# First rows of the experts gathered, and their down weights loaded, in the last steps of the attention: a transformer block on one Trainium2 core

## The reference

```python
xn = layernorm(x)                      # x: 4 x 1024 tokens, 256 wide, float32
# attention: 16 heads of 16, causal, with ALiBi bias
q, k, v = xn @ Wq, xn @ Wk, xn @ Wv
w = softmax((where(causal, q @ k.T, -1e30) + slope * (j - i)) / sqrt(16))
attn = (w @ v) @ Wo + bo
# experts: 8 of them, each token goes to its best 2
logits = rms_normalised(xn) @ router_logits
choices = top2(logits); weights = softmax(logits) / sum of the chosen
h = gelu(xs @ w_gate[e]) * (xs @ w_up[e])       # xs: rows sorted by expert, hidden width 256
ffn = sum over the token's 2 choices of weight * scale[e] * (h @ linear[e])
out = x + attn + ffn
```

## Time and profile before

| what | us |
|---|---|
| median of 3 runs | 894.63 (894.17 to 898.16) |
| the profiled execution | 894.28 |
| its span, first to last instruction | 892.5 |
| PE, DVE, ACT, POOL busy | 816.1, 555.9, 491.2, 397.1 |
| mean granted clock of PE | 0.965 |

### The profile page before, as it was taken

How to read it: one execution, slowest core, us unless ns; L and a number is a source line. 1 busy time by engine, 2 the same in 40 slices (tenths; PEclk the granted TensorE clock), 3 DMA queues, 4 the chain that set the end, 5 groups by cost and what they waited for, 6 DMA issues and landing times. The chain is left out here.

```text
span 892.5 us, 17183 instructions
## 1 busy us (share of the span) xinstructions
PE 816.1 (91%) x5618; PEld 422.1 (47%) x5619; DVE 555.9 (62%) x1560; ACT 491.2 (55%) x1011; POOL 397.1 (44%) x478
## 2 busy tenths in 40 slices
PE   4999878999998999999999999849999999999598
PEld 2555413334443344444444444315556555565597
DVE  4777399999999988888888887002222222222287
ACT  1444303777776777777877777823333333333374
POOL 6666301111211245433555421234666666665397
PEclk9999957999999999999999999969999999999699
DMA  8899767766535775567665500056222222222485
GB/s 195 275 290 279 248 84 94 90 72 84 65 50 59 85 100 84 84 87 110 85 91 84 70 2 7 1 169 226 83 86 84 82 83 87 82 85 68 143 251 186
DMA packets 93631, 100.25 MB, mean 112 GB/s; under 512 B 32700, under 2 KB 74300, under 8 KB 93500
## 3 DMA queue, kind: packets, MB, share of 16 engines
q1 hardware_dynamic: 84600, 80.40, 45.8%
q0 software_dynamic: 8960, 18.95, 6.8%
HBM read 63.89 MB, written 35.00 MB: 111 GB/s over the span
## 5 line engine op out<-in xcount | busy, mean ns | idle before, releaser
L825 ACT ACTIVATE probs<-spsum 128x512 f32<-128x512 f32 x576 | 317.5, 602 | 145.1 <-PE spsum L898 138.3
L664 DVE CUSTOM_DVE_ANT_0 junk<-mpsum,mask 128x128 bf16<-128x128 f32 (+7 forms) x512 | 359.1, 754 | 45.3 <-issue 29.6
L872 PE MATMUL mpsum<-ks,qs 102*128 102x512 bf16 (+3 forms) x768 | 183.7, 343 | 28.6 <-DVE maxima L664 22.0
L898 PE MATMUL spsum<-qs,ks 105*128 105x512 bf16 (+3 forms) x768 | 198.1, 329 | 4.8 <-ACT probs L825 3.4
L644 POOL TENSOR_SCALAR_AFFINE_SELECT probs<-probs 128x512 f32<-128x512 f32 x128 | 79.2, 638 | 252.6 <-ACT probs L825 252.3
L918 PE MATMUL cpsum<-probs,vs 128*17 128x256 f32 (+2 forms) x2560 | 154.0, 361 | 1.5 <-POOL probs L644 0.8
L1100 PE MATMUL gu<-w_gu,xTs 128*128 x288 | 137.4, 600 | 1.7 <-ACT xTs L1044 1.7
L1079 DVE COPY hT<-hp 128x256 f32<-128x256 f32 x72 | 30.6, 425 | 165.8 <-PE hp L1107 165.8
L872 PEld LDWEIGHTS mpsum<-ks,qs 102*128 102x128 bf16 x768 | 67.5, 100 | 111.7 <-DVE maxima L664 55.4
L898 PEld LDWEIGHTS spsum<-qs,ks 105*128 105x128 bf16 x768 | 66.9, 97 | 90.8 <-ACT probs L825 39.2
L1019 POOL DMA_INDIRECT expert_rows<-y,places x72 | 70.8, 984 | 69.9 <-ACT y L1053 69.6
(11 more groups left out here) (122 smaller groups left out, 708.5 us busy)
## 6 DMA issues: line engine op xcount, KB each, us to landing
qk_parts<-ctxT SPq DMA_DIRECT2D x32, 384.0 KB, 3.6
qs<-qk_parts SPq DMA_DIRECT2D x96, 128.0 KB
ks<-qk_parts SPq DMA_DIRECT2D x96, 128.0 KB
yk<-expert_rows SPq DMA_DIRECT2D x32, 256.0 KB, 3.0
v_rows<-ctxT SPq DMA_DIRECT2D x8, 544.0 KB, 3.6
vs<-v_rows SPq DMA_DIRECT2D x16, 272.0 KB, 11.0
ctxT<-in_x SPq DMA_DIRECT2D x8, 512.0 KB, 6.2
xn_rows<-ctxT SPq DMA_DIRECT2D x8, 512.0 KB, 5.7
```

The costliest lines, as they stand in the source:

```text
L664: last = dve.tensor_tensor_reduce(junk[:, slot, c:c + w], mpsum[:, slot, c:c + w], keep["mask"][:, S - w:S], 1.0, 3 * NEG, ALU.add, ALU.ma ...
L825: act.activation(probs[:, u % PRING, h], spsum[:, SCORE_AT["S", n, h] % SRING], ACT.Exp, scale=SCALE).then_inc(exp_done, 1)
L872: last = pe.matmul(mpsum[:, slot, at + c:at + e], qs[hq][0:R_MAX, h, qt * P:(qt + 1) * P], ks[hq][0:R_MAX, h, c:e], start=True, stop=True)
L898: last = pe.matmul(spsum[:, SCORE_AT["S", n, h] % SRING, c:c + w], ks[hq][:, h, kt * P:(kt + 1) * P], qs[hq][:, h, q0:q0 + w], start=True, ...
```

## The change

The query and key stacks of all quads become one tensor `stacks`, held for the whole program. The experts' down weights, row buffers and `y` buffers are laid in the stacks of quads 0 and 1: the down weights fill the stack of quad 0, which is read for the last time in step 12, rows and y lie in that of quad 1, read for the last time in step 13. SP loads the down weights in step 13 and the map in step 14; POOL gathers the first four tiles at the end of its attention stream, before the stage ends. AHEAD is now 4, for these gathers and for POOL's loop in `experts`, whose own first gathers are gone. The last stage's rows of x are laid in the stacks of quads 2 and 3, and its working buffers in the gate and up weights' place and over the down weights, rows and y. The diff, without the buffers of the last stage:

```diff
@@ -90,6 +90,10 @@
 SRING = 3
 
 
+RR = 4
+AHEAD = 4
+
+
 PAIRS = 2 * NU
 PV_AT = [[] for _ in range(PAIRS)]
 for _u in range(NU):
@@ -157,13 +161,13 @@
 SCORE_SEQ, SCORE_AT = score_slots()
 
 
-def head_buffers(nc, ctx):
+def head_buffers(nc, ctx, stacks):
 
     sb = lambda name, shape, dt=F32: ctx.enter_context(nc.sbuf_tensor(name, shape, dt))
     sem = lambda name: ctx.enter_context(nc.semaphore(name))
     return {
-        "qs": [sb(f"qs{i}", [ROWS, 4, S], BF16) for i in range(NQ)],
-        "ks": [sb(f"ks{i}", [ROWS, 4, S], BF16) for i in range(NQ)],
+        "qs": [stacks[0:ROWS, i, 0] for i in range(NQ)],
+        "ks": [stacks[0:ROWS, i, 1] for i in range(NQ)],
         "vs": [sb(f"vs{i}", [P, KT, 4, VW]) for i in range(NQ)],
         "stack_in": [sem(f"stack_in{i}") for i in range(NQ)],
         "v_in": [sem(f"v_in{i}") for i in range(NQ)],
@@ -515,6 +519,13 @@
             chunks(pe, body)
 
 
+def gather_rows(pool, scratch, keep, s):
+
+
+    pool.indirect_dma_start(keep["rows"][:, s % RR], None, scratch["xn"],
+                            bass.IndirectOffsetOnAxis(ap=keep["places"][:, s, 0:1].bitcast(U32), axis=0)).then_inc(keep["rows_in"][s % RR], 16)
+
+
 def attend(nc, ins, scratch, keep, heads):
@@ -603,8 +614,15 @@
                 if has(3):
                     sp.wait_ge(pv_done, PRING + NU * t)
                     load_quad(sp, scratch, heads, *quad(b, hq, 3))
+                if t == B * NQ - 3:
+                    sp.wait_ge(pv_done, PRING + NU * t)
+                    for e in range(NE):
+                        sp.dma_start(keep["w_down"][:, e * DH:(e + 1) * DH], ins["w_down"][:, e * DH:(e + 1) * DH]).then_inc(keep["w_down_in"], 16)
                 if has(1):
                     maxima_rows(t + 1, (hq + 1) % NQ)
+                if t == B * NQ - 2:
+                    sp.wait_ge(entries_out, 16 * 2 * NT)
+                    sp.dma_start(keep["places"][:, :, :].rearrange("p s c -> p (s c)"), scratch["map"].rearrange("(p s) c -> p (s c)", p=P)).then_inc(keep["places_in"], 16)
                 if t == MAP_FROM:
                     sp.wait_ge(routed, 1)
                 if MAP_FROM <= t < MAP_FROM + NE:
@@ -612,8 +630,6 @@
                     sp.dma_start(keep["w_gu"][:, e * DH:(e + 1) * DH], ins["w_gu"][:, e * DH:(e + 1) * DH]).then_inc(keep["w_gu_in"], 16)
 
             steps(sp, body)
-            sp.wait_ge(entries_out, 16 * 2 * NT)
-            sp.dma_start(keep["places"][:, :, :].rearrange("p s c -> p (s c)"), scratch["map"].rearrange("(p s) c -> p (s c)", p=P)).then_inc(keep["places_in"], 16)
 
         @block.gpsimd
         def _(pool):
@@ -646,6 +662,10 @@
 
             mask_unit(0, 0)
             steps(pool, body)
+            wait_apart(pool, pv_done, PRING + NU * (B * NQ - 2))
+            wait_apart(pool, keep["places_in"], 16)
+            for s in range(AHEAD):
+                gather_rows(pool, scratch, keep, s)
 
         @block.vector
         def _(dve):
@@ -960,26 +980,20 @@
 def experts(nc, ins, scratch, keep, last_weights):
 
 
-    RR = 4
-    AHEAD = 6
     with ExitStack() as ctx:
         sb = lambda name, shape, dt=F32: ctx.enter_context(nc.sbuf_tensor(name, shape, dt))
         sem = lambda name: ctx.enter_context(nc.semaphore(name))
         w_gu = keep["w_gu"]
-        w_down = sb("w_down", [P, NE * DH, D])
-        rows = sb("rows", [P, RR, D])
-        places, places_in = keep["places"], keep["places_in"]
+        w_down, rows, y, places = keep["w_down"], keep["rows"], keep["y"], keep["places"]
+        w_in, rows_in = keep["w_down_in"], keep["rows_in"]
         xT = sb("xTs", [P, 2, DH, P])
         gate = sb("gate", [P, 2, HID])
         hid = sb("hid", [P, 2, HID])
         hT = sb("hT", [P, 2, DH, P])
-        y = sb("y", [P, RR, D])
         tp = ctx.enter_context(nc.psum_tensor("tp", [P, 2, CH], F32))
         gu = ctx.enter_context(nc.psum_tensor("gu", [P, 2, CH], F32))
         hp = ctx.enter_context(nc.psum_tensor("hp", [P, 2, CH], F32))
         yp = ctx.enter_context(nc.psum_tensor("yp", [P, 2, CH], F32))
-        w_in = sem("w_in")
-        rows_in = [sem(f"rows_in{i}") for i in range(RR)]
         y_out = [sem(f"y_out{i}") for i in range(RR)]
         y_free, passed = sem("y_free"), sem("passed4")
         tp_ready, xT_ready = sem("tps_ready"), sem("xTs_ready")
@@ -997,8 +1011,6 @@
         @block.sync
         def _(sp):
             sp.sem_inc(y_free, RR)
-            for e in range(NE):
-                sp.dma_start(w_down[:, e * DH:(e + 1) * DH], ins["w_down"][:, e * DH:(e + 1) * DH]).then_inc(w_in, 16)
             sp.dma_start(last_weights["w_o"][:, :, :], ins["w_o"]).then_inc(last_weights["in"], 16)
             sp.dma_start(last_weights["bias"][:, :], ins["bo"].partition_broadcast(P)).then_inc(last_weights["in"], 16)
             x_rows = ins["x"].rearrange("(g p) d -> p g d", p=P)
@@ -1011,8 +1023,7 @@
 
                 if s >= RR:
                     pool.wait_ge(tp_ready, s - RR + 1)
-                pool.indirect_dma_start(rows[:, s % RR], None, scratch["xn"],
-                                        bass.IndirectOffsetOnAxis(ap=places[:, s, 0:1].bitcast(U32), axis=0)).then_inc(rows_in[s % RR], 16)
+                gather_rows(pool, scratch, keep, s)
 
             def scatter(s):
                 pool.wait_ge(y_ready, s + 1)
@@ -1024,9 +1035,6 @@
                 pool.wait_ge(y_out[s % RR], 16 * (s // RR + 1))
                 pool.sem_inc(y_free, 1)
 
-            pool.wait_ge(places_in, 16)
-            for s in range(AHEAD):
-                gather(s)
             for s in range(NST):
                 if s >= RR - 1:
                     landed(s - RR + 1)
@@ -1331,6 +1340,9 @@
             "escale": sb("escale", [P, NE]),
             "w_gu": sb("w_gu", [P, NE * DH, 2 * HID]),
             "ctxT": sb("ctxT", [P, B * NQ, S]),
+            "stacks": sb("stacks", [P, NQ, 2, 4, S], BF16),
+            "w_down_in": ctx.enter_context(nc.semaphore("w_down_in")),
+            "rows_in": [ctx.enter_context(nc.semaphore(f"rows_in{i}")) for i in range(RR)],
             "places_in": ctx.enter_context(nc.semaphore("places_in")),
             "w_gu_in": ctx.enter_context(nc.semaphore("w_gu_in")),
         }
@@ -1344,11 +1356,16 @@
         room = keep["w_gu_room"] = Room(keep["w_gu"][:, :, :].rearrange("p e h -> p (e h)"))
         keep["route"] = {"rank_of": room([P, NE]), "tile_no": room([1, NST, NE]), "reset": room([P, NE, NT]),
                          "ones": room([P, P], BF16), "tri": room([P, P], BF16)}
+        words = lambda a: a.rearrange("p i s h t -> p (i s h t)").bitcast(F32)
+        done_stacks = Room(words(keep["stacks"][:, 0:2]))
+        keep["w_down"] = done_stacks([P, NE * DH, D])
+        keep["rows"] = done_stacks([P, RR, D])
+        keep["y"] = done_stacks([P, RR, D])
         with ExitStack() as held:
-            heads = head_buffers(nc, held)
+            heads = head_buffers(nc, held, keep["stacks"])
             project(nc, ins, scratch, keep, heads)
             attend(nc, ins, scratch, keep, heads)
-        last_weights = {"w_o": sb("w_o", [P, DH, D]), "bias": sb("bias", [P, D]), "x": sb("x_rows", [P, NT, D]),
+        last_weights = {"w_o": sb("w_o", [P, DH, D]), "bias": sb("bias", [P, D]), "x": words(keep["stacks"][:, 2:4]).rearrange("p (t d) -> p t d", d=D),
                         "in": ctx.enter_context(nc.semaphore("wo_in")), "x_in": ctx.enter_context(nc.semaphore("x_rows_in"))}
         experts(nc, ins, scratch, keep, last_weights)
         combine(nc, ins, scratch, keep, last_weights, out)
```

More of the change, by code:

```diff
@@ L1152, in combine @@
     with ExitStack() as ctx:
-        sb = lambda name, shape, dt=F32: ctx.enter_context(nc.sbuf_tensor(name, shape, dt))
+        done_w = Room(keep["w_gu"][:, :, :].rearrange("p e h -> p (e h)"))
+        done_stacks = Room(keep["stacks"][:, 0:2].rearrange("p i s h t -> p (i s h t)").bitcast(F32))
         sem = lambda name: ctx.enter_context(nc.semaphore(name))
@@ L1159, in combine @@
         xr, x_in = last_weights["x"], last_weights["x_in"]
[L1160 to L1169, removed]
+        wts = done_w([P, YR, 2, 2])
+        inv = done_w([P, 2, NH])
+        ctxn = done_w([P, 2, NH, HD])
+        ctxnT = done_w([P, 2, 2, D])
+        yk = done_w([P, YR, 2, 2, D])
+        yw = done_stacks([P, 2, 2, 2, D])
+        y01 = done_stacks([P, 2, 2, D])
+        xb = done_stacks([P, 2, 2, D])
+        acc = done_stacks([P, 2, 2, D])
+        done = done_stacks([P, 2, 2, D])
         sumsT = ctx.enter_context(nc.psum_tensor("sumsT", [P, 2, CH], F32))
```

## The result

The changed kernel takes 1130.15 us at the median of 4 runs (1126.16 to 1131.85), where the kernel before takes 894.45: a ratio of 1.262, with a 95% interval from 1.257 to 1.266. The forecast was 1120, in a range of 1080 to 1180.

A forecast was written before the change was run, and what follows sets the result against it. TensorE, busy for 91% of the span, was taken as never waiting for rows in the loop. 892.5 + 199.4 - 1.3 + 1.8 = 1092.4, plus 28 for the clock, gave 1120 us; range 1080 to 1180.

The forecast's parts named there:

- AHEAD from 6 to 4: Experts' loop: the deciding term, each of 68 turns 2.93 us longer, 199.4 us in all.
- The ring: Experts' loop: row transposes, down, y, scatter, gather, landing, next row transposes in series, 6.04 us a turn instead of 3.108.
- The clock: Experts' loop: TensorE's granted clock falls in the stands; 23 low turns at 1.2 us each, 28 us.
- The likeliest case: Experts' loop: the clock goes down and up, 1120 us in all; chance 0.45.
- The waits: Experts' loop: row transposes wait for the DMA of their rows some 68 times, about 3 us each.
- The start: Start of the experts' stage: with four early gathers TensorE starts at about 594.3 rather than 595.6, 1.3 us gained.
- Down weights, map, buffers: Attention's last steps and last stage: earlier down weights load, moved map load and buffers in dead ones cost nothing.
- that the clock stays up: Rival, experts' loop: TensorE keeps its full clock despite the stands, 1092 us; chance 0.27.
- its own marker: Sign in the profile after: the granted clock in the loop should show both levels.
- that it stays down: Rival, experts' loop: the clock is low from the first stall on, 82 us more, 1174 us; chance 0.12.
- that the loop keeps its pace: Rival, experts' loop: the gather is there by the next turn, only the start counts, 888 or 893 us; chance 0.05.

The follow-up runs named there:

- the three kernels that reroute it: Changed kernel with down before the row transposes: 1059.19 us; that plus y stored before ScalarE's copy: 999.00 us; changed kernel with gather before scatter: 1059.52 us.
- 5 ahead: Changed kernel, but POOL's loop in the experts works 5 tiles ahead instead of 4: 898.26 us, ratio 1.0033 to the kernel before.
- the fillers: Changed kernel plus five extra unused matmuls on TensorE in each turn, ahead of the row transposes: 1096.66 us, ratio 1.225 to the kernel before.
- the fifth experiment: Changed kernel, but TensorE does down(s-2) before the row transposes of s+1 in each turn: 1059.19 us, ratio 1.183 to the kernel before.

## Why the prediction was right

- **AHEAD from 6 to 4** was named as the term that decides, and it is the whole loss: put back, it leaves 894.63 us; alone, in the kernel before, it makes 1134.96. The ring was put at 6.04 us a turn and measures 6.04 in the turn shown and 6.071 on the mean with the clock held up; in the turn shown 3.29 for 3.24 up to the gather, and 2.75 for 2.8 behind its start. The term, 199.4 us, measures 201.5. The estimate by the Trainium skill's page "DMA: Bandwidth & Descriptors", section "Anatomy of one DMA — SWDGE (gpsimd) path" (2.3 us for such a transfer), would have made it 27 us less; the trace has 2.7 at the median here too, and the measurement decides.
- **That it is a ring**, and not just late rows, is shown by the three kernels that reroute it without touching the lead: 5.54 for 5.57 (with the chance said above), 4.585 for 4.55, and 5.23 at the full clock for 4.74, a miss of 0.5 that was explained only from its rows. That the ring is harmless once it has two turns is shown by 5 ahead, which costs 4 us.
- **The clock** was put at 28 us, a third of the turns low at 1.2 us each, with "a choice between none and all". The likeliest case was right in kind (it goes down and up); the size is 34 us by the fillers, half the turns at about 1.0 us each (7.03 for 6.07). Too few turns at too high a price partly cancel, so that this term came within 6 us is luck. The price was too high because the low clock cost the way from the row transposes to y 0.95 us in the turn shown, where the sum took 1.2. Of the 10 us by which 1120 fell short this term is 6, the ring 2 and the start 0.7; another 0.8 is the median over the profiled execution.
- **The waits** were put at about 3 us each and are 2.35 on the mean (160.0 / 68), since TensorE's own work is longer in the turns at the low clock: 2.80 us ahead of the turn shown and 2.08 behind it.
- **The start**: 1.3 us forecast, 0.6 measured. The 6.06 us from the last indirect issue to the next stage, taken from the experts' end, are 6.90 here (587.99 to 594.89). That the early gathers delay the stage's end, as the prediction had it, is shown by moving them.
- **Down weights, map, buffers**: costed at nothing, and the kernel with the loop 6 ahead and no early gathers is at 895.69 for 895.37, the three together, not one by one. The attention's end is at 585.39 for 585.42.

The rivals: that the clock stays up was the wrong case by its own marker, the clock of 0.85 in the loop, and so was that it stays down; that the loop keeps its pace is excluded by 68 waits.

## What to carry to other kernels

The lead of a prefetch isn't how many buffers are filled at the start; it is which earlier work stands ahead of the issue in its queue, and what that work waits for. Write down the ring (consumer, work, store, issue, landing, consumer) with its durations from one turn of the trace and divide by the turns it spans: below the turn's own length it is nearly free (3.02 us under a turn of 3.11 cost 4 us in all, for single late landings), above it the turn takes its length. And a transfer issued early from a queue that ends a stage is only early if the issue itself fits into a stand of that queue; here, ahead of the last masks and not behind them, the same four gathers are worth 6 us instead of 1.

## What the runs showed that I had not expected

The time that passes between POOL's last instruction in the attention and the next stage hardly depends on how recently POOL issued its gathers. From the end of its last instruction to SyncE's start in the next stage it is 5.63 us before (last mask 584.07, start 589.70), 5.95 with the gathers as the last work (588.94 to 594.89) and 5.97 with the last gather issued ten microseconds ahead of the last mask's end (584.73 to 590.70). The two experiments without early gathers have 5.64, the six others that gather behind the last mask 5.95 to 5.96. Of the hole between the stages this part is left in every kernel here; what it consists of wasn't tried.

Useless matmuls that keep TensorE's granted clock at 1.00 made a loop faster that waits for transfers, by 34 us in 447, with the matmuls inside the ring at the full clock again. Where down was taken out of the ring (the fifth experiment), the clock fell too, to 0.90 on the mean, and cost little.
